# Second attention: where the values matmuls stand in an even step of TensorE's order

## The reference

```
x = layernorm(x)                                  # 256 x 512
y_main, y_dca = y[:, :-16], y[:, -16:]            # 240 and 16 context rows of 256
q = ln(x @ Wq + bq), k = ln(y_main @ Wk + bk), v = y_main @ Wv + bv    # 16 heads of 32, ln over a head
k_dca = ln(...), v_dca = ...                      # the same of y_dca with Wkv_dca
ctx = softmax(q k^T / sqrt(32)) v + softmax(q k_dca^T / sqrt(32)) v_dca
x = x + tanh(g) * (ctx @ Wo + bo)
```

## Time and profile before

| | |
|---|---|
| median of three runs | 3544.81 us (3540.49 to 3544.84) |
| profiled execution | 3546.12 us |
| its span, first to last instruction | 3544.4 us |
| TensorE busy | 3464.4 us, 98% |
| weight loads busy | 3000.9 us, 85% |
| VectorE / ScalarE / GpSimd busy | 65% / 53% / 38% |
| second attention | from about 2200 to 2865 us |
| granted TensorE clock, mean | 0.989 |

### The profile page before, as it was taken

One profiled execution on the slowest core, in us unless ns is written; L12 is line 12 of the kernel. 1 busy time (PEld: TensorE's weight loads), 2 busy tenths in 40 slices (PEclk: granted clock), 3 DMA queues, 4 the chain that ended last, 5 costly groups with the idle time before them and its releaser, 6 DMA issues. The chain is left out here.

```text
span 3544.4 us, 66282 instructions
## 1 busy us (share of the span) xinstructions
PE 3464.4 (98%) x22490; PEld 3000.9 (85%) x22490; DVE 2313.4 (65%) x5703; ACT 1866.7 (53%) x4822; POOL 1339.6 (38%) x1345
## 2 busy tenths in 40 slices
PE   9999999999999999899999998899999989999999
PEld 8999999999999999799999996667777668888887
DVE  6666666656666666576767778787777754545543
ACT  5555555554444444455555554787777743333332
POOL 3222222332333322254544554777777640202020
PEclk9999999999999999899999999999999999999999
DMA  4566666535666665577767764222222245344341
GB/s 166 188 237 236 236 238 237 167 98 189 236 236 233 230 235 167 184 272 251 261 250 261 259 247 143 68 89 67 64 70 64 73 128 160 110 129 126 112 131 48
DMA packets 430862, 611.00 MB, mean 172 GB/s; under 512 B 95120, under 2 KB 226320, under 8 KB 426512
## 3 DMA queue, kind: packets, MB, share of 16 engines
q1 hardware_dynamic: 330128, 394.91, 34.1%
q10 hardware_dynamic: 90208, 179.32, 13.7%
q0 software_dynamic: 10272, 33.63, 2.8%
HBM read 339.34 MB, written 268.44 MB: 171 GB/s over the span
## 5 line engine op out<-in xcount | busy, mean ns | idle before, releaser
L853 POOL TENSOR_TENSOR a_prob<-a_prob,a_rinv 128x512 f32<-128x512 f32 x256 | 266.4, 1041 | 1005.2 <-DVE a_rinv L1071 1005.2
L773 ACT ACTIVATE a_prob<-a_prob,a_low_bias 128x256 f32<-128x256 f32 x512 | 256.5, 502 | 469.7 <-DVE a_low_bias L1062 468.2
L527 PE MATMUL a_pj<-a_xt,in_hi 128*128 128x256 f32 x1024 | 309.8, 302 | 0.1
L1378 POOL TENSOR_TENSOR e_act_hi<-e_act_f,e_zeros 128x256 fp32r<-128x256 f32 x128 | 181.5, 1418 | 308.0 <-DVE e_act_f L1608 308.0
L1392 PE MATMUL e_gb<-e_xt_hi,in_hi 128*128 128x256 f32 x1024 | 291.7, 285 | 1.4 <-DVE e_xt_lo L1587 1.4
L1393 PE MATMUL e_gb<-e_xt_lo,in_hi 128*128 128x256 f32 x1024 | 290.9, 284 | 0.0
L1394 PE MATMUL e_gb<-e_xt_hi,in_lo 128*128 128x256 f32 x1024 | 290.9, 284 | 0.0
L2997 DVE TENSOR_TENSOR raw_in<-turned,raw_in 128x512 f32<-128x512 f32 x224 | 151.9, 690 | 212.5 <-PE turned L2710 209.6
L529 PE MATMUL a_pj<-a_xt,in_lo 128*128 128x256 f32 x1024 | 289.0, 282 | 0.0
L528 PE MATMUL a_pj<-a_xt,in_hi 128*128 128x256 f32 x1024 | 288.8, 282 | 0.0
L901 DVE TENSOR_TENSOR a_ot_lo<-a_avb,a_ot_hi 128x256 fp32r<-128x256 f32 x256 | 108.4, 423 | 258.2 <-ACT a_ot_hi L782 258.0
(11 more groups left out here) (478 smaller groups left out, 11299.3 us busy)
## 6 DMA issues: line engine op xcount, KB each, us to landing
raw_in<-in_w_gate SPq DMA_DIRECT2D x39, 2048.0 KB, 8.2
x_sorted<-a_spare ACTq DMA_DIRECT2D x42, 1792.0 KB
y_sorted<-a_spare ACTq DMA_DIRECT2D x42, 1792.0 KB
raw_out<-in_w_out SPq DMA_DIRECT2D x40, 1024.0 KB
in_hi<-w_ops SPq DMA_DIRECT2D x224, 128.0 KB, 2.3
in_lo<-w_ops SPq DMA_DIRECT2D x224, 128.0 KB, 2.4
raw_in<-in_x SPq DMA_DIRECT2D x32, 512.0 KB, 6.1
xt_rows<-a_xt SPq DMA_DIRECT2D x16, 1024.0 KB, 5.9
```

The source lines that it names most:

```text
L527: nc.tensor.matmul(out, a_hi, b_hi, start=start, stop=False)
L773: e = nc.scalar.activation(prob[:, u % 4, t], prob[:, u % 4, t], ACT.Exp, bias=low_bias[:, u % 2, t:t + 1], scale=-1.0, accum_out=rsum[:, ...
L853: nc.gpsimd.tensor_tensor(prob[:, u % 4], prob[:, u % 4], rinv[:, u % 2].unsqueeze(2).to_broadcast([P, 2, S]), ALU.mult).then_inc(p_done, 1)
```

## The change

In an even step the values block stood behind the first head's transposes; it now stands directly behind the scores, ahead of `turned_qk` and of both heads' transposes. The one call for the last group, `last_out` (past == 3), goes with it. All semaphores and their counts are the same.

```diff
@@ TensorE's step(i, u) @@
                 else:
                     if pair(i, u + 1):
                         scores(i, u + 1)
+                    if pair(i, u - 4):
+                        values(i, (u - 4) // 2)
+                        if past == 3:
+                            for use in ("o0", "o1"):
+                                last_out(i, u // PAIRS - 1, use, [GROUPS - 1])
                     turned_qk()
                 if pair(i, u - 2):
                     turn_p(i, u - 2, 0)
@@
                     if pair(i, u + 1):
                         scores(i, u + 1)
                 else:
-                    if pair(i, u - 4):
-                        values(i, (u - 4) // 2)
-                        if past == 3:
-                            for use in ("o0", "o1"):
-                                last_out(i, u // PAIRS - 1, use, [GROUPS - 1])
                     early()
                 late()
```

## The result

The changed kernel took 3559.37 us, the median of four runs (3557.82 to 3563.79), against 3542.65 us (four runs, 3538.79 to 3544.84: the three known before and one more) for the kernel before: a ratio of 1.0047, 95% interval 1.0035 to 1.006. It is slower by 16.7 us, outside the predicted range of 3536 to 3553. The profiled span grew from 3544.4 to 3557.6 us. The second attention accounts for all of it: from the scores in step 0 of batch 0 to the first transposes of the feed-forward it takes 687.3 us instead of 673.2.

The account below looks back on a forecast made before the run. In the second attention's full batches TensorE's chain, gaps included, was taken as the bound. Terms -9.4 + 3.9 + 0.8 + 3.9 + 1.6 = +0.8 us gave a median of 3545.6 us, range 3536 to 3553.

Parts of the forecast that it names:

- the two kinds of step without projection: Step 2, batches 1 to 4: 0.20 us later each, +0.8; step 6, batches 0 to 3 and 14: 0.77 each, +3.9.
- S: Start of the scores' loads in a step; times in us are counted from it.
- The one bank rival: ScalarE's later first-head copy delays following steps in full batches too: 3560 us; 0.13, shared with a dearer border.
- the 39 steps: Steps 0, 2 and 4 with a projection between the heads' transposes: 0.24 us gained each, -9.4 us.
- the bounds of 0.73 and 1.23: Scores' start to values' start: 0.73 is the scores' loads alone, 1.23 the drain plus the values' gap; 1.06 taken.
- The gain in steps 0, 2 and 4: With a projection, scores to the projection's second pass takes 2.75 us instead of 2.99: 0.24 gained a step.
- Step 4's 0.24: The gain in us claimed for each step 4 with a projection, batches 1 to 15.
- Step 6 with a projection: Batches 4 to 13: later query and key transposes delay the key bias and step 7's projection; 0.39 each, +3.9 us.
- The rest, +1.6: Step 4 of batch 0 and steps 0, 2, 6 of batch 15, without projection: 0.4 us each, between 0 and 0.8.
- the rival at 3530: All 62 even steps save the drain, slack absorbs delays: -15 us, 3530 us; 0.19, shared with a cheaper border.
- a border of 0.73: Scores hand over to values after 0.73 us instead of 1.06: 39 x -0.33, -13 us more, 3518 us.

Follow-up runs that it names:

- experiments 2 to 4: Kernel before, values early only in early batches' steps without projection: steps 2 and 6, step 6 alone, step 2 alone; ratios 1.0065, 1.0034, 1.0032.
- experiment 2: Kernel before with values early only in step 2 of batches 1 to 4 and step 6 of batches 0 to 3; 3572.25 us, ratio 1.0065.
- experiment 4: Kernel before with values early only in step 2 of batches 1 to 4; 3553.21 us, ratio 1.0032.
- experiment 7: Changed kernel with the old order in step 2 of batches 1 to 4 and step 6 of batches 0 to 3; 3540.26 us, ratio 0.9999.
- experiment 5: Changed kernel plus six unused matmuls in each of step 2, batches 1 to 4, and step 6, batches 0 to 3; 3543.29 us, ratio 1.0012.
- 6: Kernel before, old order, with the same six unused matmuls in each of the eight early steps without projection; 3544.76 us, ratio 1.0014.
- 8: Kernel before with values early only in step 0 of batches 1 to 14 and step 2 of batches 5 to 14; 3532.79 us, ratio 0.9983.
- experiment 1: Kernel before with values early only in steps 0 and 4 of batches 1 to 14 and step 2 of batches 5 to 14; 3533.54 us, ratio 0.9973.

## Why the prediction was wrong

The step that failed is the price of the two kinds of step without projection, +0.8 for step 2 of batches 1 to 4 and +3.9 for step 6 of batches 0 to 3 and 14. Their chains came out to a hundredth (S + 3.46 and S + 4.61, predicted 3.45 and 4.60), and at full clock so did both prices (+0.20 and +0.78 in batch 3, for 0.20 and 0.77). But the working took TensorE's clock in these batches as given, 1.00 as in rows 1, and put what a changed clock would cost at nothing without a reason. In its place, batches 1 and 2 ran some 17 us each at 1.2 GHz and cost 7.15 and 7.37 us, and batch 14 grew by 2.3 us at 0.94. Shown for the cause: the loss is there with only the early steps moved (experiments 2 to 4), it is gone with only these left out (7), and it goes when the gap is filled with work while the one bank and the order stay (5, with 6 as its control). Not separated is whether the length of the idle time or its place matters: step 2 adds only 0.2 us of it and yet, moved alone, lost 4.3 us in batch 4. Rows 10 gave a hint: a clock of 0.74 in the tail, at the end of the same stage. None of the rivals had this mechanism. The one bank rival gave 3560 us and the measurement is 3559.4, but it got there with step 6 dearer in every full batch and no gain in the 39 steps, while full batches became faster; that is a coincidence.

The other points:

- The border from scores to values, in no row before, takes 1.06 us from start to start at full clock, the value taken; the bounds of 0.73 and 1.23 were not needed.
- The gain in steps 0, 2 and 4 was right in place: scores to the second head's transposes went from 3.92 to 3.71 in step 2 and from 5.32 to 5.10 in step 0.
- Step 4's 0.24 was counted as a gain that stays. With step 6 left alone it is given back to GpSimd (8). The wait in rows 6, 0.38 where the drain behind scores takes 0.33, was a hint that these keys were already the last to come; the working didn't use it.
- Step 6 with a projection: the bias wait was predicted at near 1.2 and is 0.85, since the second head's transposes in front of it came 0.2 later too; the projection's place was right. A full batch was to take 41.22 us and takes 41.18.
- The rest, +1.6: batch 0 and the tail grew by 0.8 and 1.2, with the same mean clock in the tail (0.89). Experiments 7 and 8 suggest that the tail would have been some 5 us shorter without the moves in batch 14's step 6 and in batch 15.
- Two sums of the prediction are slightly off and change nothing: half way to the rival at 3530 is 3538, not 3536, and with a border of 0.73 that rival comes to 3517, not 3518.

The rule of the Trainium skill, TensorEngine Tiling (Array Packing), Key Properties, that a change of tiling mode drains the array held where it was tested: with one change fewer, each of steps 0, 2 and 4 became 0.21 to 0.24 us shorter. The rule of the Trainium skill, Perfetto Trace Analysis, Matmuls, on rotating PSUM banks pointed at the place that lost, and the trace agrees as to the idle time in step 6 (1.69 us in front of the second head's transposes instead of 0.93) but not in step 2 (0.97 instead of 1.03); that it would be paid at half clock afterwards it doesn't say there. The page TensorE: Matmul & The Clock Gate of the Trainium skill does, in the section A second HAM failure mode: psum-queue depth-cycling: in a kernel that cycles through PSUM banks, frequent very short idles between groups of matmuls make the clock swing between half and full, and the price is paid between the bursts. The windows above, 0.82 against 1.00, show such a swing here, with one bank and waits on its copy.

Open: why the fall comes in batches 1 and 2 but not 3 in the changed kernel, in 1 to 4 in experiment 2, in 4 alone in experiment 4, and in batch 14 of the changed kernel and experiment 7 but not of experiment 5 (39.57 us at 1.00), which has the same order there. No run here tells on what the moment depends. Nor is it shown that the better clock in the tail of experiments 1 and 8 (0.96 in both) comes of their order: each rests on one profile, and batch 0 shows that a clock can differ without one.

## What to carry to other kernels

A move that saves a drain (the time in which TensorE finishes its matmuls of one operand shape before it takes another) in the steps that are full can be worth making there alone: the versions of experiments 1 and 8 are the fastest here, while the same move in eight steps without filling work costs more than it gains in all the others. Where an order makes TensorE wait between short blocks, price not only the wait but the stretch behind it at half clock, and look whether the new gap stands among others; a few matmuls of no use can be cheaper than the gap. And a wait that is barely longer than the drain above it can be an engine already due; what was gained ahead of it in experiment 1 did not stay.

## What the runs showed of the hardware

- Gaps of 1.0 to 1.7 us among short blocks of transposes were enough for the granted clock to fall from 2.4 to 1.2 GHz, for 6.6 and 10.2 us in the two windows shown; with the gap in front of the second head's transposes filled it stayed at 1.00 (experiment 5).
- Neither the order nor the idle time of a batch says by itself whether the clock falls. Batches 1 and 3 of the changed kernel have the same instructions, and a clock of 0.82 and 0.99; batch 3 had 4.85 us without busy TensorE in 40.75, batch 1 had 4.3 in 47.40, where the matmuls at half clock last longer and hide some of it.
- Work that nobody reads can buy time: 48 matmuls brought the ratio from 1.0047 to 1.0012, where the same 48 cost the kernel before 0.14%.
- A change of operand shape costs until the last matmul of the other shape is nearly done, whichever of the other shapes follows: the next loads start 1.06 us behind scores for transposes, projections and values alike. In step 2 of batch 3 of the changed kernel the profile's modelled end of the scores is 2343.56, and the values start at 2343.49, 0.07 us before it.
